# Attention scores from two float32r parts, two heads side by side in the row halves of TensorE

## The reference

```
q = (h @ Wq.T + bq) * 8 ** -0.5      # (b, s, 16 heads, 8)
k = h @ Wk.T + bk
v = h @ Wv.T + bv
scores = einsum('bqhd,bkhd->bhqk', q, k)
out = einsum('bhqk,bkhd->bqhd', softmax(scores), v) @ Wo.T + bo
```

## Time and profile before

| | |
|---|---|
| median of 3 runs | 1086.14 us (1085.76 to 1087.13) |
| the profiled execution | 1087.2 us, its span 1085.4 us |
| attention stage | some 470 us to some 975 us of the span |
| busy share of the span | PE 88%, PEld 65%, DVE 65%, ACT 59%, POOL 65% |

### The profile page before, as it was taken

How to read it: one execution, slowest core, us unless ns; L and a number is a source line. 1 busy time by engine, 2 the same in 40 slices (tenths; PEclk the granted TensorE clock), 3 DMA queues, 4 the chain that set the end, 5 groups by cost and what they waited for, 6 DMA issues and landing times. The chain is left out here.

```text
span 1085.4 us, 29610 instructions
## 1 busy us (share of the span) xinstructions
PE 956.3 (88%) x9809; PEld 706.1 (65%) x9810; DVE 704.7 (65%) x1509; ACT 641.7 (59%) x1304; POOL 703.8 (65%) x1531
## 2 busy tenths in 40 slices
PE   6999997669899999449999999999999999954675
PEld 5888886458777666335767777777777777623554
DVE  5888887634444444237788777778878777825752
ACT  4777775311124433125788888888888888752551
POOL 4777775466625555467688888888888887544003
PEclk9999999789999999757999999999999999987999
DMA  8600000311122332134344544454454444302000
GB/s 319 252 3 3 3 3 2 121 45 42 42 70 82 82 84 65 44 109 132 116 140 138 149 127 140 125 147 137 139 141 129 125 124 128 102 16 61 7 3 20
DMA packets 88836, 100.90 MB, mean 93 GB/s; under 512 B 10654, under 2 KB 74366, under 8 KB 88318
## 3 DMA queue, kind: packets, MB, share of 16 engines
q1 hardware_dynamic: 83454, 87.98, 27.5%
q0 software_dynamic: 5248, 11.15, 3.2%
HBM read 61.79 MB, written 36.47 MB: 91 GB/s over the span
## 5 line engine op out<-in xcount | busy, mean ns | idle before, releaser
L1367 DVE TENSOR_REDUCE a_neg_max<-a_slot 128x4 f32<-128x1024 f32 x256 | 306.7, 1219 | 109.0 <-PE a_slot L1510 84.3
L1455 ACT ACTIVATE a_pT<-a_slot 128x1024 f32<-128x1024 f32 x256 | 255.4, 1024 | 14.0 <-PE a_slot L1526 7.1
L1510 PE MATMUL a_slot<-a_k_stack,a_q_stack 72*128 72x256 bf16 x1024 | 158.3, 279 | 7.3 <-DMA a_k_stack<-part_dram 6.5
L1526 PE MATMUL a_slot<-a_q_stack,a_k_stack 75*128 75x256 bf16 x1024 | 150.8, 275 | 2.6 <-ACT a_pT L1455 0.7
L1541 PE MATMUL a_ps_o<-a_pT,a_v_pad 128*32 128x256 f32 x2048 | 141.6, 386 | 0.0
L1510 PEld LDWEIGHTS a_slot<-a_k_stack,a_q_stack 72*128 72x128 bf16 x1024 | 95.7, 99 | 51.8 <-issue 25.5
L727 POOL DMA_INDIRECT y_rows<-m_total,m_token x80 | 76.6, 957 | 68.7 <-issue 40.4
L1526 PEld LDWEIGHTS a_slot<-a_q_stack,a_k_stack 75*128 75x128 bf16 x1024 | 92.8, 98 | 36.4 <-ACT a_pT L1455 14.3
L720 POOL DMA_INDIRECT sorted_in<-h,m_slot x64 | 62.6, 978 | 42.5 <-issue 24.0
L330 DVE TENSOR_TENSOR r_score<-ps_score,r_decay 128x512 f32<-128x512 f32 x128 | 81.5, 678 | 7.9 <-PE ps_score L489 7.8
L1541 PEld LDWEIGHTS a_ps_o<-a_pT,a_v_pad 128*32 128x32 f32 x2048 | 64.8, 109 | 27.5 <-issue 13.0
(11 more groups left out here) (296 smaller groups left out, 2113.6 us busy)
## 6 DMA issues: line engine op xcount, KB each, us to landing
a_q_stack<-part_dram SPq DMA_DIRECT2D x64, 288.0 KB
a_k_stack<-part_dram SPq DMA_DIRECT2D x64, 288.0 KB
part_dram<-a_part SPq DMA_DIRECT2D x64, 192.0 KB, 2.7
sorted_in<-h SPq DMA_DIRECT2D x10, 528.0 KB, 13.0
m_xe<-sorted_in SPq DMA_DIRECT2D x40, 132.0 KB
expert_up<-in_eu_dram SPq DMA_DIRECT2D x1, 4096.0 KB, 24.2
part_dram<-a_part SPq DMA_DIRECT2D x64, 64.0 KB, 3.8
out_dram<-e_x_plus_h SPq DMA_DIRECT2D x32, 128.0 KB, 2.5
```

Source lines behind the costliest of these rows:

```text
L1367: nc.vector.tensor_reduce(neg_max[:, p, half, t, g * UNIT:(g + 1) * UNIT], slots[SLOT_OF["m", j]][:], AX.X, ALU.max, negate=True).then_inc ...
L1455: nc.scalar.activation(pT[:, j % PT_RING], slots[SLOT_OF["e", j]][:], ACT.Exp).then_inc(e_read, 1)
L1510: ins = nc.tensor.matmul(slots[SLOT_OF["m", j]][:, q], q_stack[0:QK_ROWS, p, half, head, t * P:(t + 1) * P], k_stack[0:QK_ROWS, p, half, h ...
L1526: ins = nc.tensor.matmul(slots[SLOT_OF["e", j]][:, q], k_stack[0:EXP_ROWS, p, half, head, t * P:(t + 1) * P], q_stack[0:EXP_ROWS, p, half, ...
```

## The change

q and k are split into two float32r parts each (`PARTS` = 2), so there are four products of parts and a head needs 4 x 8 = 32 rows (`QK_ROWS`). The array's rows are used as two halves (`TILES` = 2, `TILE_ROWS` = 64): of each unit's four heads two lie in rows 0 to 63 of the stacks and two in rows 64 to 127, and `scores` issues the matmuls of both halves in turn. Each half writes its own bank of the slot. The maximum's two parts stand in rows 62 and 63 of each half; rows 32 to 61 are filled with zeros once, in both stacks (in `k_stack` rows 62 and 63 with ones), so a maximum matmul takes 62 rows and an exponential matmul 64. The stacks are float32 now, 4 heads x 256 x 4 bytes = 4 KB a row of a half, as before (8 heads x 256 x 2 bytes).

`split` has two POOL instructions instead of four. The parts are stored to two tensors in HBM, `q_dram` (one transfer a half) and `k_dram` (one transfer for each part and half, since there the part is an inner dimension). A fill is four transfers a half: q and k for each tile. `give_max` is two transfers a half. DVE's reduction writes its four maxima in the order of the tiles.

```
-PARTS = 3
+PARTS = 2
...
-EXP_ROWS = QK_ROWS + PARTS
+TILES = 2
+TILE_ROWS = P // TILES
+MAX_ROWS = TILE_ROWS - PARTS
+HT = HH // TILES
...
-        FILLS = 2
+        FILLS = 2 * TILES
+        STORES = 1 + PARTS
...
             def store_parts(s, p, r):
-                slots = lambda half, first, end: part_dram[p, half, first:end].rearrange("a d h s -> (d h) a s")
-                rows = lambda half: part[half * HH * AD:(half + 1) * HH * AD, p].rearrange("r w a s -> r (w a) s")
-                after(sp, part_step, 8 * s + 4)
+                rows = lambda half, which: part[half * HH * AD:(half + 1) * HH * AD, p, which]
+                after(sp, part_step, 2 * PARTS * s + PARTS)
                 for half in range(HALVES):
                     after(sp, filled[p][half], twice(8 * FILLS, r))
-                    sp.dma_start(slots(half, 2 * PARTS, SLOTS), rows(half)[:, PARTS:2 * PARTS - 1]
+                    for a in range(PARTS):
+                        sp.dma_start(k_dram[p, half, :, a], rows(half, 1)[:, a]
+                                     ).then_inc(part_stored[p][half], 16)
+                after(sp, part_step, 2 * PARTS * (s + 1))
+                for half in range(HALVES):
+                    sp.dma_start(q_dram[p, half].rearrange("a d h s -> (d h) a s"), rows(half, 0)
                                  ).then_inc(part_stored[p][half], 16)
-                after(sp, part_step, 8 * (s + 1))
-                for half in range(HALVES):
-                    sp.dma_start(slots(half, 0, 2 * PARTS), rows(half)).then_inc(part_stored[p][half], 16)
...
-                    after(sp, part_stored[p][half], twice(16, r + 1))
-                    sp.dma_start(q_stack[0:QK_ROWS, p, half],
-                                 part_dram[p, half, 0:PARTS].rearrange("a d h s -> (a d) (h s)").unsqueeze(1)
-                                 .to_broadcast([PARTS * AD, PARTS, HH * S])).then_inc(filled[p][half], 16)
-                    sp.dma_start(k_stack[0:QK_ROWS, p, half],
-                                 bass.AP(part_dram.tensor, part_dram[p, half, PARTS].offset,
-                                         [[HH * S, PARTS * AD], [AD * HH * S, PARTS], [1, HH * S]])
-                                 ).then_inc(filled[p][half], 16)
+                    after(sp, part_stored[p][half], 16 * STORES * (r + 1))
+                    for tile in range(TILES):
+                        rows, heads = slice(tile * TILE_ROWS, tile * TILE_ROWS + QK_ROWS), slice(tile * HT, (tile + 1) * HT)
+                        sp.dma_start(q_stack[rows, p, half],
+                                     q_dram[p, half, :, :, heads].rearrange("a d h s -> (a d) (h s)").unsqueeze(1)
+                                     .to_broadcast([PARTS * AD, PARTS, HT * S])).then_inc(filled[p][half], 16)
+                        sp.dma_start(k_stack[rows, p, half],
+                                     k_dram[p, half, :, :, heads].rearrange("d a h s -> (d a) (h s)").unsqueeze(0)
+                                     .to_broadcast([PARTS, PARTS * AD, HT * S])).then_inc(filled[p][half], 16)
...
-                    sp.dma_start(q_stack[QK_ROWS:EXP_ROWS, p, half], max_T[:, half]).then_inc(max_in[p][half], 16)
+                    for tile in range(TILES):
+                        at = tile * TILE_ROWS
+                        sp.dma_start(q_stack[at + MAX_ROWS:at + TILE_ROWS, p, half],
+                                     max_T[tile * PARTS * HT:(tile + 1) * PARTS * HT, half]).then_inc(max_in[p][half], 16)
...
+                nc.gpsimd.tensor_tensor(high.bitcast(F32R), value, none, ALU.add).then_inc(steps, 1)
+                after(pool, steps, at + 1)
+                nc.gpsimd.tensor_tensor(low.bitcast(F32R), value, high, ALU.subtract).then_inc(steps, 1)
...
+            def scores(slot, rows, weights, moving, of_weights, p, half, g):
+                for r in range(UT):
+                    for tile in range(TILES):
+                        at = slice(tile * TILE_ROWS, tile * TILE_ROWS + rows)
+                        ins = nc.tensor.matmul(slot[:, tile * UT + r], weights[at, p, half, g * UT + r, of_weights].bitcast(F32R),
+                                               moving[at, p, half, g * UT + r].bitcast(F32R), start=True, stop=True)
+                return ins
```

More of the change, by code:

```diff
@@ L11 @@
 BF16 = mybir.dt.bfloat16
+F32R = mybir.dt.float32r
 I32 = mybir.dt.int32
@@ L1280, in step @@
                         for half in range(HALVES):
-                            after(pool, part_stored[p][half], twice(16, r))
-                    split(part_step, 8 * s + 4 * n, qk[:, p, which], rest[:, which], part[:, p, which, 0],
-                          part[:, p, which, 1], part[:, p, which, 2], [P, S])
+                            after(pool, part_stored[p][half], 16 * STORES * r)
+                    split(part_step, 2 * PARTS * s + PARTS * n, qk[:, p, which], part[:, p, which, 0], part[:, p, which, 1], [P, S])
                 return step
@@ L1289, in step @@
                     after(pool, maxT_done, HALVES * (s - 1) + half + 1)
[L1290 to L1291 removed]
+                    tiles = lambda a: a.rearrange("p t c h -> p (t c) h")
+                    split(max_step, 2 * PARTS * s + PARTS * half, neg_max[:, p, half].rearrange("p t c g r -> p (t c) (g r)"),
+                          tiles(max_part[:, half, :, :, 0]), tiles(max_part[:, half, :, :, 1]), [P, TPS * TILES, HT])
                 return step
@@ L1504, in step @@
                 def step(s, p, r):
+                    if j == 0 and isinstance(s, int) and s == 0:
+                        pe.wait_ge(ones_in, 16 * 2 * TILES)
                     if j % 4 == 0:
@@ L1507, in step @@
                     free_slot("m", j, s)
-                    for q in range(UNIT):
-                        head = g * UNIT + q
-                        ins = nc.tensor.matmul(slots[SLOT_OF["m", j]][:, q],
-                                               q_stack[0:QK_ROWS, p, half, head, t * P:(t + 1) * P],
-                                               k_stack[0:QK_ROWS, p, half, head], start=True, stop=True)
-                    ins.then_inc(m_filled, 1)
+                    scores(slots[SLOT_OF["m", j]], MAX_ROWS, q_stack, k_stack, slice(t * P, (t + 1) * P), p, half, g
+                           ).then_inc(m_filled, 1)
                 return step
@@ L1518, in step @@
                 def step(s, p, r):
-                    if j == 0 and isinstance(s, int) and s == 0:
-                        pe.wait_ge(ones_in, 16 * 2 * HALVES)
                     if j % 4 == 0:
-                        after(pe, max_in[p][half], 16 * (r + 1))
+                        after(pe, max_in[p][half], 16 * TILES * (r + 1))
                     free_slot("e", j, s)
-                    for q in range(UNIT):
-                        head = g * UNIT + q
-                        ins = nc.tensor.matmul(slots[SLOT_OF["e", j]][:, q],
-                                               k_stack[0:EXP_ROWS, p, half, head, t * P:(t + 1) * P],
-                                               q_stack[0:EXP_ROWS, p, half, head], start=True, stop=True)
-                    ins.then_inc(e_filled, 1)
+                    scores(slots[SLOT_OF["e", j]], TILE_ROWS, k_stack, q_stack, slice(t * P, (t + 1) * P), p, half, g
+                           ).then_inc(e_filled, 1)
                 return step
@@ L1632, in by_half @@
 def by_half(weight):
-    return np.ascontiguousarray(weight.reshape(-1, HALVES, HH, AD).transpose(0, 1, 3, 2).reshape(-1, D))
+    heads = weight.reshape(-1, HALVES, HH // UNIT, TILES, UT, AD)
+    return np.ascontiguousarray(heads.transpose(0, 1, 5, 3, 2, 4).reshape(-1, D))
 def by_pair(rows):
```

70 lines of the change are left out of this document (33 added, 37 removed).

## The result

The changed kernel takes 1208.4 us (median of 4 runs, 1201.4 to 1211.6) where the kernel before takes 1086.6 beside it: a ratio of 1.110, with a 95% interval of 1.105 to 1.116. The forecast was 1155 with a range up to 1200. The direction is right and so is the place, but the loss is 122 us and not 68.

What follows compares the result with a forecast made beforehand. Two DMA engines carrying the k fills were to bound the kernel: 15.5 us of work plus 1.3 us drain, a 16.8 us period against 14.7. Over 32 sequences 67 us, plus 1 at the start, on 1087.2: 1155 us, range 1098 to 1200.

Steps and rivals of the forecast that it cites:

- What bounds the stage: Attention stage: two DMA engines carrying the k fills set a period of 16.8 us a sequence; given 62%.
- The reading of the outermost counts from three shares: DMA: a transfer uses the largest count up to 16 dividing both sides' outermost counts; k fills get 2 engines.
- The sum of the two engines, 15.5 us: Work a sequence on the two DMA engines: k fills 10.2 us, the rest other fills, stores, maxima, output and loads.
- the drain step: The two DMA engines have only leftovers until stores land and a new k fill is issued: 1.3 us, 0 to 2.7.
- The start and the end: Outside the steady sequences: first k fill 2.5 to 4 us later, first split up to 2.6 shorter, so +1 us.
- The clock: Rival: TensorE, working in pieces, runs half the time at 1.2 GHz; period 18.5 us, 1209 us; 5%.
- SP, 14.8 us: SP's transfer issues a sequence: 19 instead of 11, at 0.63 to 0.65 or 0.78 us plus 0.05 each; ends 9.3 and 16.9.
- k fill spreads: Rival: k fills use more engines and SP's issues set the pace, 15.2 us a sequence, 1103 us; 15%.
- TensorE, 12.3 us: TensorE's work a sequence: 14.7 us, less 3.5 for paired scores, plus 1.1 for changes of tile shape.
- the count of 18: TensorE's changes of tile shape a sequence after the change, against 8 before.
- 10 x 0.11: TensorE: price of ten more changes of tile shape a sequence at 0.11 us on average, 1.1 us.
- POOL, 9.4 us: POOL's work a sequence after 3.4 us less of splitting; beside TensorE's work, so worth nothing by itself.

Runs made afterwards that it cites:

- wide_k: The changed kernel with the parts stored in one tensor as before, so a k fill has 16 outermost source rows, not 2: 1079.7 us, ratio 0.992.
- half_narrow: The changed kernel with only the second tile's k fills issued as two fills of 16 rows each: ratio 1.016, period 15.21 us.
- before_narrow: The kernel before with stack rows reordered so q and k fills have an outermost source count of 3 instead of 24: 1262.6 us, ratio 1.159.
- busy_wait: The changed kernel with six throwaway matmuls ahead of each of TensorE's two waits a sequence for a fill: 1195.9 us, ratio 1.097.
- k_in_two: The changed kernel with each k fill issued as two fills of 16 rows, 23 SP issues a sequence instead of 19: 1117.2 us, ratio 1.026.
- the added matmuls: wide_k with one more matmul at four places a sequence between score units, over 128 rows or over 64: 1130.8 and 1091.7 us.
- full_rows_b: wide_k with each of the 64 score matmuls a sequence taking all 128 rows, one after the other, for time alone: ratio 1.024, period 15.63 us.

## Why the forecast was wrong, step by step

**What bounds the stage: right.** TensorE's waits for the k fill, the share of two in 16, and pairs 0.11 to 0.12 us apart were foretold, and wide_k, half_narrow and before_narrow show the cause. Two signs came out otherwise: SP was to be nearly without idle time and waits 91 of 300 us, and TensorE is busy 84% and not 75%, since its list is longer than summed (14.5 us in wide_k) and longer still at the low clock. The reading of the outermost counts from three shares held in every run. The Trainium skill (DMA: Bandwidth & Descriptors, Rules for kernel authors) names this very form: a leading zero-stride broadcast of c copies confines a transfer to at most c engines; the trace agrees, 0.13 for c = 2, 0.19 for c = 3. Its other rule, that two transfers to disjoint partition halves serialize, decided nothing: wide_k keeps the split, its k fills land 2.8 us after their issue, and they are no bound.

**The sum of the two engines, 15.5 us: the first step that failed.** Counted packet by packet, two or more packets are in flight for 277 of the 300 us, 16.8 us a sequence, and fewer than two for 23 us, 1.4 us a sequence. (The trace doesn't number the engines, so 16.8 us is the two engines' work at most.) Against the forecast that is 1.3 us more of work and 0.1 us more of idle time than the 1.3 us of the drain step, which was good; SP's waits for its own stores, 22.7 us in 300, are the same 1.4 us. The packets were the mis-sized term. I priced them by their length when a queue runs alone: 0.159 us for 4 KB, which is the median after too. But their mean is 0.198 us: 0.175 while about two are in flight, 0.21 to 0.22 while nine or more are. And now and then packets stand for 0.5 to 1.4 us (at 627.4 us two took 1.1). How much belongs to each isn't settled. 32 x 1.4 is 45 of the 53 us that are missing.

**The start and the end.** I had +1 us; the first four sequences cost 5 us above their share of the steady loss, the end 3. The first is 4 us above my +1, so with 45, 4 and 3 the 53 us are accounted for but for one.

**The clock: a term made into a rival.** I gave a slower clock 5% as a case of its own, at 18.5 us a sequence. It is no other case: it follows from the waits of the likeliest one, had shown a low clock at 440 us, and work in the waits gave 12 us back. These lie within the 1.4 us above and don't come on top of them: in busy_wait fewer than two packets are in flight for 1.2 us a sequence instead of 1.4, and two or more for 16.7 instead of 16.8. That the measured 1208 lies beside that rival's 1209 is chance, since at the full clock the period is 17.9 us.

**SP, 14.8 us: mis-sized, without effect.** A wrong rule from few rows: 32-row fills cost 0.6 us, and k_in_two gives 13.1 us for 19 issues. The rival "k fill spreads" would have come out as wide_k, 1080 us, and not 1103.

**TensorE, 12.3 us: the second step that failed**, hidden in the changed kernel and laid bare by wide_k at 14.5. The float32r pair is one pass, as taken; in a run it takes 0.12 us and not 0.11 (+0.3 us a sequence). The transposes of the maxima in float32, "under 0.1 us each" and left out of the sum, cost 0.47 us more than before. A good part of it are changes of shape that the count of 18 hadn't: from such a transpose to the values behind it TensorE takes 0.20 us in wide_k and 0.04 in before (medians of the steps from start to start), twice a sequence, so 0.3 us. And the other changes of shape, by subtraction, cost 2.5 us where 10 x 0.11 stood: 1.9 in the scores and 0.6 in the other work. This is more than the added matmuls priced: ten changes at 0.16 are 1.6 us, TensorE's waits in wide_k are 0.3, and 0.6 us stay open. Six of the eight old changes have half-height units beside them now and may have grown dearer; no run priced them. The price was taken from changes next to the values. The earlier trace rows held a dearer one, 1.07 us for four groups of 0.22, so 0.19 for the change, and I used that row for the groups alone. Of a saving of 7.0 - 3.8 = 3.2 us this leaves 0.2, which is the period's 14.68 to 14.48.

**POOL, 9.4 us: right.** In wide_k it is busy 194 of 300 us, 9.4 us a sequence, and it gained nothing, as said.

**The range** was too narrow at its upper end: its 18.2 us for the period is what was measured, but above that it allowed nothing for the start and the end, which took 5 and 3 us.

## What to carry to other kernels

Look at the outermost count of both sides of every transfer before anything else: a broadcast in front of the rows puts it on as many engines as it has copies, and the work of those few engines, not the mean DMA share (0.35 here), is what to add up. Half the rows at twice the rate pays only for long runs of the same tile shape; count the changes, at 0.16 us each by the added matmuls and up to 0.27 by full_rows_b, before counting matmuls. And when a forecast has waits of microseconds in front of TensorE, put the low clock behind them into its sum.

## What the runs showed of the hardware

- Two float32r matmuls of 64 rows and 256 columns in the two row halves start 3 ns apart (median in wide_k) and take 0.12 us together; one over 128 rows (full_rows_b) takes the same 0.12 us. Their weight loads take 183 to 190 ns each and are hidden in a run of such work.
- Across a change of tile shape two starts are 0.20 to 0.21 us apart in wide_k, and the second pair of score matmuls behind it comes after 0.22 us instead of 0.12.
- In the wait of 3.6 us from 702.95 us on the granted clock was still 1.00; it was the 6.8 us of work behind it that ran at 0.50.
- Added matmuls whose results are thrown away made a kernel faster, by 1.2%.
- Four of SP's issues more went with a faster stage (18.21 to 15.87 us), because the k fills then went to 16 engines instead of two.
- With wide fills the changed kernel beats the kernel before by 0.8% (0.9912, 0.9924 and 0.9928 in three comparisons). No run went below that.
